# A fused attention and mixture-of-experts kernel: weights work of TensorE issued ahead of its waits, in place of keep-warm products

## What is computed

```python
x = x + xattn(ctx, ctx, layernorm(x))             # softmax(q k^T / sqrt(128)) v, with Wq Wk Wv Wo
h = layernorm(x); xt = h.reshape(-1, 128)
p = softmax(xt @ Wr + br); probs, idx = top_k(p, 2); probs /= probs.sum(-1)
h = LN(relu(xt @ W1[e] + b1[e]), g1[e], be1[e])   # W1: 8 x 128 x 512
y = LN(relu(h @ W2[e] + b2[e]), g2[e], be2[e])    # W2: 8 x 512 x 128
out = x + sum over the two chosen e of gate_e * y_e
```

## Time and profile before

| | us |
|---|---|
| median of 3 runs | 274.54 (273.24 to 274.83) |
| the profiled execution | 272.01 |
| its span in the profile | 270.1 |
| mean granted clock of PE in it | 0.956 |

### The profile page before, as it was taken

How to read it: one execution, slowest core, us unless ns; L and a number is a source line. 1 busy time by engine, 2 the same in 40 slices (tenths; PEclk the granted TensorE clock), 3 DMA queues, 4 the chain that set the end, 5 groups by cost and what they waited for, 6 DMA issues and landing times.

```text
span 270.1 us, 10311 instructions
## 1 busy us (share of the span) xinstructions
PE 234.5 (87%) x2961; PEld 192.8 (71%) x2964; DVE 232.9 (86%) x1098; ACT 214.1 (79%) x799; POOL 189.1 (70%) x301
## 2 busy tenths in 40 slices
PE   1999679999697497778779999999999999999990
PEld 1566567767575344778668999999999999999330
DVE  0768986955989988789979899999999999999893
ACT  2557476779879867868799999999999999999700
POOL 8704277777757777828768877788888888888640
PEclk9999985999999669999999999999999999999997
DMA  6998596133325134455332333233415697441357
GB/s 165 314 288 294 128 311 219 41 99 96 124 81 166 53 104 95 91 132 82 75 77 70 73 84 71 63 81 61 89 45 140 151 196 168 114 104 60 102 169 249
DMA packets 48803, 34.59 MB, mean 128 GB/s; under 512 B 26934, under 2 KB 42870, under 8 KB 48747
## 3 DMA queue, kind: packets, MB, share of 16 engines
q1 hardware_dynamic: 39100, 22.83, 32.0%
q0 software_dynamic: 6592, 9.00, 12.6%
q10 hardware_dynamic: 3056, 2.11, 2.7%
HBM read 15.14 MB, written 12.02 MB: 101 GB/s over the span
## 4 chain that ended last, share of the span: by engine, by line
DVE 36%; issue 22%; PE 15%; ACT 11%; DMA 7%; DVEq 4%; POOL 1%; SPq 1%; POOLq 1%; ACTq 1%
PE bank L729 9%; DVE vo L1915 7%; PE bank L733 4%; DMA w2f<-in_L_ffn_W 3%; DVE rs L1956 3%; DVE cx L1945 3%; DVE kq L1908 3%; DVE w2f L1676 3%; DVEq L1922 2%; DVE st L1933 2%; ACT ex L1183 2%; DMA w2f<-answers 2%; DVE mv L1939 1%; POOL answers L687 1%; ACT rh L1355 1%
## 5 line engine op out<-in xcount | busy, mean ns | idle before, releaser
L687 POOL DMA_INDIRECT answers<-vo,words_of x71 | 70.0, 986 | 26.6 <-issue 17.3
L675 POOL DMA_INDIRECT slot_rows<-pay,pos x64 | 64.2, 1004 | 29.0 <-issue 18.5
L729 PE MATMUL bank<-kb_room,w1h 128*128 128x128 f16 x568 | 55.2, 219 | 1.8 <-issue 1.8
L733 PE MATMUL bank<-w2h,rh 128*128 x284 | 51.4, 219 | 2.7 <-ACT w2l L1130 1.6
L733 PE MATMUL bank<-rh 128*128 128x129 f16 x284 | 51.5, 220 | 0.0
L733 PE MATMUL bank<-w2l,rh 128*128 x284 | 51.4, 219 | 0.0
L729 PE MATMUL bank<-kb_room,w1l 128*128 128x128 f16 x284 | 51.2, 219 | 0.0
L1908 DVE SCALAR_TENSOR_TENSOR kq<-bank,rh 128x512 f16<-128x512 f32 x71 | 47.8, 673 | 0.1
L729 PEld LDWEIGHTS bank<-kb_room,w1h 128*128 x568 | 43.6, 98 | 2.6 <-issue 2.6
L1355 ACT ACTIVATE rh<-bank 128x512 f16<-128x512 f32 x71 | 41.1, 579 | 4.2 <-PE bank L729 3.8
L733 PE MATMUL bank<-w2h,kq 128*128 x284 | 40.3, 222 | 4.5 <-DVE kq L1908 3.7
(11 more groups left out here) (269 smaller groups left out, 601.4 us busy)
## 6 DMA issues: line engine op xcount, KB each, us to landing
x_tok<-in_x SPq DMA_DIRECT2D x8, 256.0 KB, 6.9
w1f<-in_L_ffn_W SPq DMA_DIRECT2D x2, 1024.0 KB, 9.3
pay<-pay SPq DMA_DIRECT2D x8, 256.0 KB, 3.0
w1f<-answers SPq DMA_DIRECT2D x8, 256.0 KB
w2f<-answers SPq DMA_DIRECT2D x8, 256.0 KB, 3.6
kb_room<-slot_rows SPq DMA_TRANSPOSE x71
words_of<-slot_rows POOLq DMA_DIRECT2D x71, 1.0 KB
answers<-vo,words_of POOLq DMA_INDIRECT x71
```

The lines of the kernel that those rows point to most:

```text
L675: eng.indirect_dma_start(slot_words, bass.IndirectOffsetOnAxis(ap=pos[:, g % 2, k, i:i + 1], axis=0), pay[g % 2][:, k, i, :].bitcast(U32), ...
L687: eng.indirect_dma_start(answers, bass.IndirectOffsetOnAxis(ap=words_of[:, j % NW, 0:1], axis=0), z[j % NZ], None).then_inc(s_ans[j % NZ], 16)
L729: return eng.matmul(dst, lhsT, rhs, start=start, stop=stop)
L733: return eng.matmul(dst, lhsT, rhs, start=start, stop=False, skip_group_check=True)
```

## The change

In PE's order, `values(1)` moves from the end of pass 2 to ahead of `keep(10)` and `probT(2)`. `w_rows(0, 0)`, `w_rows(1, 0)`, `w_rows(1, 1)` and `up_low(0)` move from the end of passes 3, 4, 5 and 6 to ahead of `ranks` in the same pass, and there they take the place of that pass's second `keep(10)`. `up_low(1)` moves from the end of pass 7 to ahead of `keep(10)` and `probT(7)`. `w_rows(0, 1)`, `values(2)` and `up_low(2)` stay at the end of their passes. Forty keep-warm products of 142 in the loop fall away; all else is as it was, and no other engine's order changes.

```diff
                 if n < GROUPS:
+                    if n == 2:
+                        values(1)
+                    elif n == 7:
+                        up_low(1)
                     keep(10)
                     probT(n)
...
-                    keep(10)
+                    if n == 3:
+                        w_rows(0, 0)
+                    elif n in (4, 5):
+                        w_rows(1, n - 4)
+                    elif n == 6:
+                        up_low(0)
+                    else:
+                        keep(10)
                     ranks(n - 1)
                 if n < GROUPS - 2:
                     xT_(n + 2)
                 if n < GROUPS - 1:
                     skip(n + 1)
-                if n == 2:
-                    values(1)
                 if n == 3:
-                    w_rows(0, 0)
                     w_rows(0, 1)
-                if n == 4:
-                    w_rows(1, 0)
                 if n == 5:
-                    w_rows(1, 1)
                     values(2)
-                if n == 6:
-                    up_low(0)
                 if n == 7:
                     places(0)
-                    up_low(1)
                     up_low(2)
```

## The result

The changed kernel is slower: 279.74 us median of 6 runs (278.04 to 282.39) against 275.41 us of the kernel before (6 runs, 273.24 to 278.38). The ratio is 1.020 with a 95% interval of 1.015 to 1.025. The profiled execution took 278.81 us.

What follows compares the result with a forecast made beforehand. Of the edited places only pass 3 was taken to lie on the path, through PE: +1.65 us on the profiled 272.01 gave 273.7, plus about half the 2.5 us to the runs' median, 275.0 us; range 272.5 to 277.8.

Steps and rivals of the forecast that it cites:

- `values(1)` fills the wait before `probT(2)` and opens one before `probT(3)`: Pass 2: the moved work fills PE's 1.66 us wait, and PE then waits 4.6 us for `prob(3)`.
- The fall behind it, 10.24 us: After the wait before `probT(3)`: PE's clock falls at about 45 us and stays low until 55.3 us, near certain.
- The price in pass 3, +1.65 us: Pass 3: PE's work at the low clock puts `probT(4)` at 60.7 us instead of 59.05; bounds +0.9 to +2.5 us.
- the second route: Pass 3: late `ranks(2)` delays DVE's `nmax` and `prob(4)` to about 60.1 us, 0.6 us behind PE, adding nothing.
- Passes 5 and 6, costed as "free": `w_rows(1, 1)` at 1.8 us and `up_low(0)` at 1.07 us fit into PE's waits ahead of `ranks`, cost 0.
- the absence of the forty products: Passes 4 to 6: leaving out these keep-warm products costs nothing, covered by a wait or by late ACT and DVE.
- Pass 4, 0 and up to 0.7 us: `w_rows(1, 0)` delays `ranks(3)` by some 2.2 us; cost 0 under DVE's 2.84 us idle time, up to 0.7 without it.
- "`probT(2)` late because `values(1)` overruns": Pass 2: listed sign of a wrong forecast, which had 1.6 us of work filling a 1.66 us wait nearly exactly.
- Pass 7: the wait before `probT(7)` didn't stay.: Claimed: the 1.99 us wait and its fall stay, the wait before `ranks(7)` grows to about 1.7 us, gain 0.
- Rival C: A late fall at 103 to 105 us hits `down_low(2)`, `down_low(3)` and the first tiles: 278.8 us; chance 0.13.
- The price by the Trainium skill: Low stretch in the first part: throttled time times (1 - 1.2/2.4), which alone would make 5.1 us.

Runs made afterwards that it cites:

- e1: Kernel before with only `values(1)` and `up_low(1)` moved ahead of `probT(2)` and `probT(7)`; 277.34 us median, ratio 1.010.
- e5: Changed kernel with keep-warm products sized to every wait of PE from pass 1 to pass 8; 276.26 us median, ratio 0.999 to the kernel before.
- e4: Changed kernel with 85 instead of 10 keep-warm products ahead of `probT(3)`; 278.12 us median, ratio 1.008 to the kernel before.
- e7: Changed kernel with the forty removed products put back behind the moved work, ahead of `ranks`; 280.81 us median, ratio 1.019 to the kernel before.
- e3: Kernel before with the forty keep-warm products ahead of `ranks` in passes 3 to 6 left out, nothing moved; 278.77 us median, ratio 1.015.
- e9: Kernel before with all 142 keep-warm products of the first part left out, nothing moved; 277.02 us median, ratio 1.005.
- e12: Changed kernel with waits filled by resized keep-warm products and `up_low(1)` back at the end of pass 7; 275.48 us median, ratio 1.001 to the kernel before.
- e6: Kernel before with keep-warm products sized to every wait of PE in passes 1 to 8, nothing moved; 275.33 us median, ratio 1.005.

## Why the prediction was wrong

The range ended at 277.8 us and the median is 279.74. The direction of the sum was right (+1.65 us), its size was not: 4.3 us between the medians, 4.9 and 7.0 us from `prob(3)` to the first tile in the two pairs of profiles.

- **`values(1)` fills the wait before `probT(2)` and opens one before `probT(3)`: right.** Predicted 4.6 us; 3.84, 4.38 and (e1) 4.61 us were measured.
- **The fall behind it, 10.24 us: right** in the first profile (48.3 to 58.5 us) and in e1 (10.2 us); 13.6 us in the second profile. It began 3.3 us after the wait's begin in the first profile, 2.8 in the second and 2.7 in e1, where I had 2.6 to 3.2. The kernel before shows 10.24 us twice and nothing else; that it would be 10.24 us again was a guess that came true twice in three.
- **The price in pass 3, +1.65 us: right in kind, somewhat small.** Counted from `prob(3)`, PE came to `probT(4)` 1.9 us later than in the kernel before in the first profile, 3.0 us in the second, 1.6 us in e1. More of the low stretch lay behind `probT(3)` than I had put there (9.7 and 12.1 us instead of 8.6), and with the measured stretches in it my own sum comes within 0.5 us of each. In the first profile 0.3 us more comes by the second route, which the prediction had set at 0.6 us behind: `ranks(2)` late, `pick` waiting 4.30 us, `prob(4)` at 62.32, and ACT, through with its wait for PE, waiting 0.15 us more for DVE's `nmr`. In the second profile the wait for PE ended last.
- **Passes 5 and 6, costed as "free": the step that failed.** I costed `w_rows(1, 1)` at 1.8 us and `up_low(0)` at 1.07 us, full-clock durations, against waits that they fit into. Both ran at the low clock (3.3 us, 2.2 us) and no longer fitted; `ranks` came late, DVE stood at `picked`, and each pass lost 1.1 to 1.6 us. I let the clock fall once on the path, computed that one, and took the other places at full speed. e5 shows that the costing was right at the full clock, e4 that it fails where the clock is low. Of the 4.9 us of the first profile 2.6 come from here, where the prediction had 0. Whether the absence of the forty products was rightly put at nothing stays open: put back behind the moved work they gave nothing (e7, 1.019), the kernel before without them was 1.5% slower (e3), without all 142 0.5% (e9).
- **Pass 4, 0 and up to 0.7 us:** 0 in the first profile, 1.4 us in the second, by the same step. `values(1)` is a third place of that kind: costed at 1.6 us against a wait of 1.66, it ran at the low clock in e4 and e7 and cost 1.9 us ahead of `prob(3)`. "`probT(2)` late because `values(1)` overruns" was one of the prediction's own signs of being wrong.
- **Pass 7: the wait before `probT(7)` didn't stay.** It was 1.00 and 0.90 us instead of 1.99, and the wait before `ranks(7)`, put at 1.7 us, is not there. Neither costs anything: 18.77 and 18.65 us to the first tile.
- **The profile as a base: misleading.** The profiled execution, 272.01 us, is faster than every other one of this kernel: the 87 executions beside the experiments lie between 272.20 and 281.50 us, median 276.5. The prediction had half seen it. Among these 87 the time goes with the time at the low clock, worked out from each one's mean granted clock and span (correlation 0.93, 0.34 us for each us; 23 to 48 us low each): 274.0 us on the mean under 28 us, 279.4 us above 38 us. That is a relation among executions of one kernel, and e9 shows that it doesn't carry to another.
- **Rival C** had the time (278.8 us) but not the place: no fall hit `down_low(2)`, `down_low(3)` and the first tiles. The stretch from 99.5 to 109.7 us ended just ahead of them, and from `prob(7)` to the first tile the changed kernel takes 18.77 us, as before. The time came out by luck.
- **The price by the Trainium skill** (page "TensorE: Matmul & The Clock Gate", section "HAM oscillation — how this bites in real kernels"), half of a low stretch or an estimate of 5.1 us for 10.2, is met in no run here: 10.2 us low cost 0 us under the W2 transfer (kernel before), 1.6 us in e1, 2.2 us with `w_rows(0, 0)` in front of `ranks` (changed kernel).

## What to carry to other kernels

In this kernel work moved ahead of a wait was free only at the clock at which it had been measured. Where the profile shows an engine's clock changing, cost the moved work at both levels against the wait it must fit, and look at what the next wait becomes when one is filled. Filler products are not interchangeable with real work ahead of a signal that another engine waits for: in pass 5 a filler of 0.56 us at the full clock still fitted when it took twice that, a weights step of 1.8 us did not, and neither did the 46 products of e5 ahead of `ranks(7)`. And when single executions of a kernel scatter by 3%, profile it more than once before using one profile as the base of a sum.

## What the runs showed of the hardware

- A low stretch lasted from 3.4 us (75.6 to 79.0 in the changed kernel) to 13.7 us (48.1 to 61.8 in e3), where the profile of the kernel before had shown 10.24 us twice.
- The clock also fell where PE had hardly waited. In e12 it fell at 16.8 us. PE's last wait had been 0.30 us long and had ended at 12.54 us, and PE was busy from there on:

```profile
14.00:16.00 2.00, 2.00 (x12) 1.26 (x10) 0.71 (x4) 0.13 (x1) 0.00 (x0) 1.00 1.05 399
16.00:18.00 2.00, 2.00 (x12) 1.87 (x12) 1.03 (x6) 1.99 (x9) 0.00 (x0) 0.71 1.13 257
```

  Eleven of the 14 profiles have a low stretch of 3.4 us that begins ahead of 24 us, at different places, though all kernels issue the same up to about 26 us. The two profiles of the kernel before, without it and with it, differ by 1.4 us at `prob(3)`. What sets its place stays open.
- Holding the clock up for all of the first part (e6, none low in the profile) narrows the executions, 274.61 to 278.27 us against 272.20 to 281.05, more than it lowers their median.
